# The causal mask of the attention weights, put by POOL's selects on the exponentials in place of PE's matmuls on the scores

## The reference

```python
scores = jnp.einsum('bth,bsh->bts', q, k) * Cd ** (-0.5)
causal = jnp.tril(jnp.ones((Td, Td), dtype=bool))
scores = jnp.where(causal, scores, -jnp.inf)
attn = jax.nn.softmax(scores, axis=-1)
out = jnp.einsum('bts,bsh->bth', attn, v)
```

## Time and profile before

| | |
|---|---|
| median of 3 runs | 131.51 us (130.37 to 131.53) |
| span of the profiled execution | 130.9 us |
| PE busy | 118.2 us, 90% of the span |
| DVE, ACT, POOL busy | 81.7, 49.7, 49.6 us |
| mean granted TensorE clock | 0.959 of full speed |

### The profile page before, as it was taken

The page is one execution under the profiler, slowest core; times in us unless marked ns, Lnnn a source line. Parts: engine busy times, 40 slices in busy tenths (PEclk is TensorE's granted clock), DMA queues, the critical chain, the costliest instruction groups (busy, mean ns, idle before and its releaser), DMA issues.

```text
span 130.9 us, 2520 instructions
## 1 busy us (share of the span) xinstructions
PE 118.2 (90%) x943; PEld 83.6 (64%) x943; DVE 81.7 (62%) x276; ACT 49.7 (38%) x125; POOL 49.6 (38%) x70
## 2 busy tenths in 40 slices
PE   5999979999999968989987999999988999999950
PEld 2453546676876667759743865776765445999930
DVE  6379499388669878986895139717847947000063
ACT  3111173061071164145150632364294256566620
POOL 6158049720088193899575715050050001000000
PEclk9999999999999999995999599689999999999999
DMA  3530000000000000000000000000000000000027
GB/s 49 93 52 3 0 8 0 0 0 5 0 0 3 0 5 0 0 0 5 3 3 0 0 0 5 0 0 0 5 0 0 0 0 0 5 0 0 0 36 124
DMA packets 9213, 1.32 MB, mean 10 GB/s; under 512 B 9170, under 2 KB 9202, under 8 KB 9202
## 3 DMA queue, kind: packets, MB, share of 16 engines
q1 hardware_dynamic: 9202, 1.17, 5.7%
HBM read 0.64 MB, written 0.52 MB: 9 GB/s over the span
## 4 chain that ended last, share of the span: by engine, by line
PE 63%; DVE 18%; ACT 9%; issue 4%; POOL 4%; POOLq 0%; DVEq 0%
PE bank L891 7%; PE bank L1315 6%; PE bank L1011 6%; PE bank L1304 5%; ACT eqk L446 5%; PE bank L1038 5%; PE bank L977 5%; PE bank L1105 4%; PE bank L1121 3%; PE bank L1137 3%; POOL ln_rs L397 3%; PE bank L1112 2%; PE bank L984 2%; DVE z L689 2%; PE bank L1164 2%
## 5 line engine op out<-in xcount | busy, mean ns | idle before, releaser
L397 POOL TENSOR_TENSOR ln_rs<-ln_ve,halfneg 128x8 f32<-128x8 f32 x10 | 16.4, 1647 | 24.6 <-DVE ln_ve L699 24.6
L891 PE MATMUL bank<-idle_b 128*128 128x512 bf16 x67 | 20.3, 421 | 1.5 <-DVE idle_b L590 1.5
L446 ACT ACTIVATE eqk<-bank 128x512 f32<-128x512 f32 x16 | 8.3, 602 | 11.9 <-PE bank L996 11.9
L1304 PE MATMUL bank<-wxn,ident 128*128 128x124 f32 (+3 forms) x60 | 11.6, 277 | 0.2 <-DVE wxn L855 0.2
L891 PEld LDWEIGHTS bank<-idle_b 128*128 128x128 bf16 x67 | 6.6, 106 | 7.6 <-issue 2.1
L1038 PE MATMUL bank<-ctxo,eqk 128*128 128x132 f32 x64 | 10.8, 304 | 0.5 <-DVE ctxo L676 0.3
L861 DVE TENSOR_TENSOR out_tok<-bank,t 128x256 f32<-128x256 f32 x4 | 1.4, 415 | 14.4 <-PE bank L1327 14.4
L1038 PEld LDWEIGHTS bank<-ctxo,eqk 128*128 128x128 f32 x64 | 8.7, 201 | 2.2 <-issue 1.0
L1304 PEld LDWEIGHTS bank<-wxn,ident 128*128 128x128 f32 x60 | 9.5, 194 | 0.9 <-DVE wxn L855 0.7
L1105 PE MATMUL bank<-uT,tnT 32*128 32x256 f32 (+1 forms) x64 | 8.9, 388 | 0.6 <-DVE smax_b L724 0.5
L1315 PE MATMUL bank<-warm,vT_bd 128*128 128x124 f32 (+3 forms) x48 | 9.3, 274 | 0.0
(11 more groups left out here) (185 smaller groups left out, 250.8 us busy)
## 6 DMA issues: line engine op xcount, KB each, us to landing
x_tok<-in_x_dram SPq DMA_DIRECT2D x8, 64.0 KB, 2.3
out_dram<-out_tok SPq DMA_DIRECT2D x4, 128.0 KB, 2.6
w_raw<-in_L_conv_w_qkv_dram SPq DMA_DIRECT2D x1, 48.0 KB, 2.3
wout_sb<-in_L_conv_w_out_dram SPq DMA_DIRECT2D x1, 16.0 KB
brow<-in_L_conv_b_out_dram SPq DMA_DIRECT2D x1, 0.1 KB
gln_bc<-in_L_conv_g_ln_dram SPq DMA_DIRECT2D x1, 16.0 KB, 2.5
bln_bc<-in_L_conv_b_ln_dram SPq DMA_DIRECT2D x1, 16.0 KB, 2.9
w_raw<-in_L_attn_Wq_dram SPq DMA_DIRECT2D x1, 4.0 KB, 2.0
```

Source lines behind the costliest of these rows:

```text
L397: pool.tensor_tensor(ln_rs[:, n, r], ln_ve[:, n, r], halfneg[:], ALU.pow).then_inc(s_rs[n], 1)
L446: act.activation(eqk[:, r, g], bank[g][:], ACT.Exp).then_inc(s_expA, 1)
L891: pe.matmul(bank[at][:], idle_b[:, 0:P], idle_b[:], start=True, stop=True)
L1304: pe.matmul(part(c, s)[:, :, j0:], ident[:], wxn[:, m, c * RPC:(c + 1) * RPC, j0 + at:CHUNKS + at], start=True, stop=False)
```

## The change

`masks(r)` and its constant `mask_st` are removed. In their place POOL clears the diagonal blocks of the exponentials: for each sequence g of a round it waits for `s_expB`, and one `affine_select` over 128 x (2 x 128) f32 elements, in place in `eqk`, keeps an element where the query is not before the key and writes 0.0 elsewhere. It signals the new semaphore `s_probs`, and PE's `values` waits for that in place of `s_expB`. The four groups of four selects stand in POOL's list after `heads(3)`, after `power(0, 3)`, after `power(2, 0)` and after `power(2, 1)`. The mask of the maxima (`mask_ts`) stays.

```diff
--- before.py
+++ after.py
@@ -104,7 +104,6 @@
         sel4 = sb("sel4", [P, G, P], BF16)
         sel8 = sb("sel8", [P, 8, P], BF16)
         mask_ts = sb("mask_ts", [P, P], BF16)
-        mask_st = sb("mask_st", [P, P], BF16)
 
 
         gn_stats = sb("gn_stats", [P, R, 6])
@@ -233,6 +232,7 @@
         s_shB = sem("s_shB")
         s_st = sem("s_st")
         s_expB = sem("s_expB")
+        s_probs = sem("s_probs")
         s_pv = sem("s_pv")
         s_pvT = sem("s_pvT")
         s_pvk = sem("s_pvk")
@@ -377,8 +377,6 @@
             link(select(sel8[:], ALU.not_equal, 1.0, 0, [[-1, 8], [0, P]]))
             link(pool.memset(mask_ts[:], 0.0))
             link(select(mask_ts[:], ALU.is_ge, MASKED, 0, [[-1, P]]))
-            link(pool.memset(mask_st[:], 0.0))
-            link(select(mask_st[:], ALU.is_ge, MASKED, 0, [[1, P]], -1))
             link(pool.memset(groupavg[:], 0.0))
             for g in range(G - 1):
                 link(select(groupavg[:], ALU.not_equal, 1.0 / G, -C * g, [[0, G], [-1, C]]))
@@ -401,6 +399,13 @@
                     link(pool.tensor_tensor(zg[:, r], zg[:, r],
                                             ln_rs[:, 0, r][:, :, None].broadcast_to([P, G * HALVES, C]), ALU.mult))
                     pool.tensor_tensor(t1[:, r], zg[:, r], xb[:, r], ALU.add).then_inc(s_t1, 1)
+
+            def causal(r):
+
+                for g in range(G):
+                    pool.wait_ge(s_expB, r * G + g + 1)
+                    diagonal = eqk[:, r, g].rearrange("p (k q) -> p k q", k=2)[:, :, 0:P]
+                    select(diagonal, ALU.is_ge, 0.0, 0, [[0, 2], [1, P]], -1).then_inc(s_probs, 1)
 
             heads(0)
 
@@ -413,11 +418,15 @@
             power(1, 1)
             power(0, 2)
             heads(3)
+            causal(0)
             power(1, 2)
             power(0, 3)
+            causal(1)
             power(1, 3)
-            for r in range(2):
-                power(2, r)
+            power(2, 0)
+            causal(2)
+            power(2, 1)
+            causal(3)
             pool.wait_ge(s_bnve, 1)
             pool.tensor_tensor(bn_sc[:, 1:2], bn_sc[:, 0:1], halfneg[:, 0:1], ALU.pow).then_inc(s_bnrs, 1)
             pool.memset(state[:, :, 0:STRIDE - 1], 0.0).then_inc(s_kept, 1)
@@ -1106,12 +1115,6 @@
                               rows(uT, g)[:, r, ks * P:TW], start=(ks == 0), stop=True,
                               skip_group_check=(ks == 1))
 
-            def masks(r):
-                for g in range(G):
-                    for ks in range(HALVES):
-                        pe.matmul(bank[g][:, 256 * ks:256 * ks + P], ident_b[:], mask_st[:],
-                                  start=False, stop=True, skip_group_check=True)
-
             def shifts_b(r):
                 pe.wait_ge(s_shB, r + 1)
                 for g in range(G):
@@ -1132,7 +1135,7 @@
                     pe.wait_ge(s_shB, R)
                 pe.wait_ge(s_v1, r + 1)
                 for g in (2 * b, 2 * b + 1):
-                    pe.wait_ge(s_expB, r * G + g + 1)
+                    pe.wait_ge(s_probs, r * G + g + 1)
                     for ks in range(HALVES):
                         ins = pe.matmul(vbank[r][64 * (g % 2):64 * (g % 2) + 64, b * TW + ks * P:(b + 1) * TW],
                                         v1[:, r, ks, g, :], probsT[:, r, g, 256 * ks:TW + ks * P],
@@ -1228,7 +1231,6 @@
             pe.wait_ge(s_v1, 1)
             pe.wait_ge(s_shB, 1)
             contexts(3)
-            masks(0)
             shifts_b(0)
             outs(3, (0, 1))
             for r in range(R):
@@ -1273,7 +1275,6 @@
                         keep_awake("turn 2", at=7)
                     if r + 2 < R:
                         turn(r + 2)
-                    masks(r + 1)
                     shifts_b(r + 1)
             values(3, 1)
             turn_2(1)
```

## The result

The change is slower: 135.34 us median of 4 executions (134.47 to 138.71) against 130.94 for the kernel before (130.25 to 131.53). The ratio is 1.0352, with a 95% interval of 1.0275 to 1.0429. The prediction was 132.0 with a range up to 133.5.

What follows compares the result with a forecast made beforehand. PE, busy 90% of the span, was taken to set the length where nothing holds it up. Terms +2.2 - 0.2 - 1.64 - 0.2 - 0.6 = -0.44 us of gain, so 131.5 + 0.44, rounded 132.0 us; range 130.2 to 133.5.

Steps and rivals of the forecast that it cites:

- the term for the clock: Behind PE's new wait in round 3 the clock more likely than not falls, costing up to 1.6 us; 0.6 taken.
- the faster rival: Selects at 311 ns, gain from removed masks near 2.7 us, no clock fall behind the wait: 129.9 us, chance 0.13.
- a different count of stretches at half clock: Sign of being wrong in the profile after: the number of slow-clock stretches on PE differs from before.
- within 0.5 us of 96.45: Sign of being right: the transpose `values_back(2)` in the profile after starts this close to its earlier start.
- G: Time gained on the chain up to round 3 by removing masks 0 to 2: 2.2 us, bounds 1.8 and 2.7.
- Selects: Sixteen on POOL, 0.42 us each, four in 1.7 us; round 0's push back the power by 0.2, rounds 1 and 2 nothing.
- The wait of `values(3, 0)`: In round 3 PE waits behind `power(2, 1)` and two selects, with `values_back(2)` queued behind: costs 1.64 us.
- The idle time of PE in front of it: Before the first select of round 3 ends, PE stands idle for 2.2 us.
- Ports: DVE's `normalize(2, 1)` gets between two selects of round 3, lasting 0.8 us; the second select comes later, 0.2 us taken.
- the rival in which POOL always wins: DVE is shut out for all four selects, pushing back round 3's maxima: 132.5 us, chance 0.12.
- slower, the tail: Round 3's `values(3, 0)` waits behind `power(2, 1)` and two selects, outweighing the gain from removed masks: 133.2 us, chance 0.22.

Runs made afterwards that it cites:

- none: The changed kernel without its selects, so no causal mask is put on the weights at all: 133.51 us median.
- last_pe: The changed kernel with selects in rounds 0 to 2 only and round 3 masked by PE as before: 133.83 us median.
- pads: `none` plus 8 idle bf16 matmuls of 128 x 128 where each group of masks stood: 131.28 us median, ratio to before 1.0009.
- both: The changed kernel with the masks put back on PE and all selects kept: 132.36 us median, ratio to before 1.0112.
- last_only: The changed kernel with selects in round 3 alone and PE's masks in rounds 0 to 2: 134.22 us median.
- order: The changed kernel with round 3's selects ahead of `power(2, 1)` on POOL and `normalize(2, 1)` behind `attend(2)` on DVE: 132.48 us median.
- pad1: `last_pe` plus 8 idle matmuls of 128 x 128 where the masks of round 1 had stood: 131.51 us median, ratio to before 0.9999.
- pad2: `last_pe` plus 8 idle matmuls of 128 x 128 where the masks of round 2 had stood: 132.0 us mean.

## Why the prediction was wrong

The step that failed is the term for the clock. It stood in the sum with 0.6 us, for one more fall behind PE's wait in round 3. In its place the runs showed 9.5 us more at half clock on average (19.5 against 10.0), at 0.36 us each 3.4 us of time. The larger part needs no wait on POOL: `none` and `last_pe`, which have none, have 18.0 and 17.8 us. It comes from the removed matmuls themselves, and `pads` and `both` show that matmuls of the same size in their places undo it. The prediction named this only as a reason against the faster rival ("less work on PE beside the same waits speaks for more falls of the clock") and gave it no price and no chance of its own. The profile of before had a hint: all three groups on the chain ran at half clock, the one of round 1 by the earlier trace rows, behind 0.8 us of waiting, those of rounds 0 and 2 by two more stretches of the same view, and the kernel already ran 67 idle matmuls to hold the clock.

```profile
58.70:62.10 3.40, 3.40 (x27) 3.21 (x26) 2.33 (x10) 1.64 (x4) 3.23 (x3) 0.51 0.02 5
...
82.59:86.00 3.41, 3.41 (x32) 2.92 (x30) 2.07 (x7) 2.09 (x6) 0.60 (x1) 0.51 0.00 0
```

Of the signs of being wrong that the prediction named, "a different count of stretches at half clock" is the one that came, and `values_back(2)` started at 101.59 in the profile, not within 0.5 us of 96.45.

The Trainium skill's page "TensorE: Matmul & The Clock Gate", section "Part 1: The HAM clock gate", says that the throttled clock is the default and that activity of the engine releases it. The runs agree: `none` and `pads` differ in activity alone, by 18.0 and 9.9 us at half clock.

The sum without the clock term was too good as well: forecast was a gain of 0.16 us, measured at equal clock is a loss of 1.3. What the masks were worth was mis-sized, and so was the wait beside it. By terms:

- Removed masks: G was taken as 2.2. `none`, which has no selects, measured 1.3 (± 0.4), under the lower bound of 1.8. Even that bound took the full 0.97 us for the masks of round 0, but these ran at half clock too (0.51, the first row above), which the prediction didn't look at; for the other two groups it took 0.4 each. `pads` against `none` gives 1.4 us for all four groups, 0.35 each.
- Selects: 0.42 us each were forecast; the mean is 0.44, and four take 1.5 to 1.67 us. They fitted between the heads and `power(1, 2)` as foretold, and those of rounds 0 to 2 cost 0.3 us (± 0.5) together, with the masks of round 3 (`last_pe` against `none`), beside the 0.2 taken.
- The wait of `values(3, 0)`: the place, the releaser and what was queued behind were as forecast. 1.64 us plus 0.2 for DVE was the price; `last_only` and `both` measured 1.5 and 1.2, and between `last_pe` and the changed kernel, where G is gained as in the prediction, lie 2.3 (± 0.5). The sum had it that G and the wait simply add. They don't: with the wait in place, leaving out the masks gained nothing at equal clock (`both` +1.2, changed +1.3), where without it `none` gained 1.3. Why wasn't tried apart.
- The idle time of PE in front of it: 2.2 us forecast, 2.39 in the profile; and the clock did fall behind it there, but not in the profiles of `both` and `last_only`.
- Ports: `normalize(2, 1)` was to last 0.8 us and took 0.61. The second select took 0.59 us where the others took 0.41, so it ended 0.2 us later, which is the term of 0.2. DVE went on between the first two selects, and the rival in which POOL always wins didn't happen. By the page "SBUF — State Buffer" of the Trainium skill, section "Who interferes with whom", the second to start is blocked for the whole instruction of the first; the select of 0.41 us from 99.12 had 0.34 us to go when `normalize` began at 99.19, and this lost 0.19, so less than that.
- The rival "slower, the tail" (133.2, chance 0.22) had a right mechanism for a part of the loss: `order`, which mends the tail and puts no matmul back, is 3.7 us faster than the changed kernel on the mean, 1.8 of it at equal clock. Without the clock that the removed matmuls had held it stopped 2 us short.

Against the mean of 131.4 us the account is +1.3 at equal clock and +3.4 for the clock, together the measured 136.1 - 131.4 = 4.7. That it closes is no test, since the fit makes it so.

## What to carry to other kernels

Before removing matmuls from PE, look at the granted clock next to them: where stretches at half clock lie near and PE waits between its steps, cheap dense matmuls may hold the clock that the expensive ones run at; here the 32 removed ones were worth about as much as they cost (`pads` 131.4 and `none` 133.0 us on the mean, with a standard error of 1.1 on the difference), so removing them gained nothing. Price that by a run with idle matmuls in their places, and compare kernels at equal clock as well as by their means. Where a small operation is moved to another engine, look at its last instance first: here that was the one which nothing hid.

## What the runs showed of the hardware

- One us at half clock cost 0.36 us of time on average in this kernel (0.29 to 0.43 by single variants), and one kernel's executions ranged from 4 to 21 us at half clock (before) and 7 to 27 (changed).
- 8 bf16 matmuls of 128 x 128 in one place (`pad1`), 0.8 us (± 0.5) at equal clock, took 8 us (standard error 2.9) off the time at half clock (17.8 to 9.8); with the same in the next round instead (`pad2`) it was 14.0.
- One idle matmul of 128 rows by 256 columns between f32 matmuls on 32 rows lengthened each step from 0.55 to 0.84 us, at a granted clock of 1.00 in both.
- POOL's select over 128 x 256 f32 took 0.41 us alone; beside a DVE operation with two inputs one of four took 0.59, and DVE's took 0.61 in place of 0.42.
